# Sixteen-head attention with a mixture of experts: the token stage with the next block's K matmuls between gate/up and down, V and the shift copied by ScalarE, and V stored in rows of 4 KB

## What is computed

```
xn = layernorm(x)                                # no affine part
q, k, v = split(xn @ W_qkv.T + b_qkv)            # 16 heads of 16
probs = softmax(q k^T / 4 - slope_h * |i - j|)
s = (probs @ v) @ W_out.T + b_out
g = silu(routed(xn) + shared(xn))                # 2 of 8 experts, router on xn; one shared expert
shared(xn) = (silu(xn @ sw_gate) * (xn @ sw_up)) @ sw_down
x + s * g
```

## Time and profile before

| | us |
|---|---|
| median of 3 runs (lowest, highest) | 2485.53 (2479.53, 2488.43) |
| the profiled execution: its own time | 2477.84 |
| its span, first to last instruction | 2476.1 |
| the token stage, to the first instruction of the next | 370.6 |
| the attention stage | 370.6 to 2338.8 |
| the output stage | 2338.8 to 2476.1 |
| busy in the span: PE, ACT, DVE, POOL | 2051.5, 1792.6, 1007.1, 549.8 |

### The profile page before, as it was taken

The page is one execution under the profiler, slowest core; times in us unless marked ns, Lnnn a source line. Parts: engine busy times, 40 slices in busy tenths (PEclk is TensorE's granted clock), DMA queues, the critical chain, the costliest instruction groups (busy, mean ns, idle before and its releaser), DMA issues. The chain is left out here.

```text
span 2476.1 us, 41361 instructions
## 1 busy us (share of the span) xinstructions
PE 2051.5 (83%) x15921; PEld 723.3 (29%) x15922; DVE 1007.1 (41%) x2375; ACT 1792.6 (72%) x2080; POOL 549.8 (22%) x577
## 2 busy tenths in 40 slices
PE   4688875676799999999999999999999998788565
PEld 2345542111122224222222332222224221111154
DVE  6676656411133335333333443333335332444255
ACT  3444444566798888888888888888888887888610
POOL 1222220566401111111111111111111104555022
PEclk9888886878899999999999999999999998989888
DMA  9766664554323325332333443233335323433296
GB/s 305 232 212 215 214 204 110 147 155 143 116 74 92 98 78 142 96 86 84 95 96 85 111 114 98 79 94 92 91 87 136 102 63 81 120 103 105 56 285 219
DMA packets 212584, 316.75 MB, mean 128 GB/s; under 512 B 81744, under 2 KB 156112, under 8 KB 212128
## 3 DMA queue, kind: packets, MB, share of 16 engines
q1 hardware_dynamic: 172064, 197.63, 29.1%
q0 software_dynamic: 31872, 108.03, 14.4%
q10 hardware_dynamic: 8448, 8.39, 1.0%
HBM read 196.25 MB, written 125.83 MB: 130 GB/s over the span
## 5 line engine op out<-in xcount | busy, mean ns | idle before, releaser
L1203 ACT ACTIVATE probs_att<-SC_att 128x1024 f32<-128x1024 f32 (+10 forms) x1776 | 1578.0, 956 | 289.0 <-PE SC_att L1093 205.5
L1116 PE MATMUL O_att<-probs_att,V_att 128*32 128x512 f32 (+6 forms) x8192 | 954.1, 535 | 17.1 <-DVE probs_att L1229 15.8
L1093 PE MATMUL SC_att<-Q_att,K_att 64*128 64x512 f16 (+6 forms) x4332 | 654.9, 341 | 241.1 <-ACT probs_att L1203 168.5
L1229 DVE TENSOR_TENSOR probs_att<-probs_att,decay_att 128x128 f32<-128x128 f32 x1024 | 293.5, 291 | 1094.6 <-ACT probs_att L1203 1012.3
L1093 PEld LDWEIGHTS SC_att<-Q_att,K_att 64*128 64x128 f16 (+1 forms) x4332 | 183.2, 94 | 1138.9 <-ACT probs_att L1203 850.2
L1116 PEld LDWEIGHTS O_att<-probs_att,V_att 128*32 128x32 f32 x8192 | 167.6, 110 | 248.6 <-issue 202.3
L1038 POOL DMA_DIRECT2D ys<-ys_att x72 | 51.5, 716 | 743.3 <-DVE ys_att L1276 743.3
L1033 POOL DMA_DIRECT2D xs_att<-xs x72 | 53.3, 740 | 445.6 <-PE TY_att L1137 431.8
L1045 POOL DMA_INDIRECT rows_in_att<-ys,place x128 | 125.5, 981 | 117.5 <-DVE gate_all L1285 83.5
L581 POOL TENSOR_TENSOR parts_tok<-qk_tok,parts_tok 128x512 f16<-128x512 f32 x64 | 78.6, 1230 | 247.0 <-ACT parts_tok L601 242.3
L1023 POOL DMA_INDIRECT xs<-rows_in_att,place x128 | 124.4, 972 | 39.6 <-issue 39.6
(11 more groups left out here) (153 smaller groups left out, 1333.2 us busy)
## 6 DMA issues: line engine op xcount, KB each, us to landing
K_att<-k_stack SPq DMA_DIRECT2D x128, 256.0 KB
Q_att<-q_stack SPq DMA_DIRECT2D x128, 256.0 KB
xs<-zero_tok SPq DMA_DIRECT2D x36, 512.0 KB, 3.8
xs_att<-xs POOLq DMA_DIRECT2D x72, 256.0 KB, 3.2
ys<-ys_att POOLq DMA_DIRECT2D x72, 256.0 KB, 2.6
k_stack<-parts_tok SPq DMA_DIRECT2D x96, 128.0 KB
q_stack<-parts_tok SPq DMA_DIRECT2D x96, 128.0 KB
x_raw_tok<-in_x SPq DMA_DIRECT2D x16, 512.0 KB, 5.7
```

What stands on the lines that cost most here:

```text
L1093: mm = pe.matmul(SC[:, c % SLOTS, at:at + x1 - x0], K[par][side or 0][rows, k * P:(k + 1) * P], Q[par][rows, x0:x1], start=True, stop=True)
L1116: mm = pe.matmul(O[VW * g:VW * (g + 1), par, col:col + width * len(mine)], V[par][:, k, :], spans[:, j0:j0 + BPB * (len(mine) - 1) + 1:BPB ...
L1203: nc.scalar.activation(probs[chunk.step % DEPTH][:, chunk.base:chunk.base + chunk.width], SC[:, c % SLOTS, start:start + chunk.width], ACT ...
L1229: v.tensor_tensor(diag, diag, decay[:, chunk.head, :], ALU.mult).then_inc(faded, 1)
```

## The change

PE runs `own(j)` ahead of `gate_up(j)`, and `k_chunks(j+1)` between `gate_up(j)` and `down(j)`. V's copy out of PSUM and the computation of the shift move from DVE to ACT. The root for block j+2 moves to the start of ACT's block, with a SiLU on one number behind it (`warm_up`); `keep_shared` moves into the next block. On DVE, `gated(j-1)` moves into block j between the two K chunks, `ln_apply` and `ln_stats` move ahead of the Q chunks, and each product follows its own Q chunk. V's bias leaves the token stage: the output stage projects it with `w_o` once, and adds the result to `b_o`. V is stored as 128 rows of 4 KB per block; the load of a head's V then reads four pieces of 256 bytes per partition, where it read one of 1 KB.

The diff, cut to its core:

```diff
@@ tokens_stage
-            (b_v[:], a["b_qkv"].rearrange("(o n) -> o n", o=1)[:, 2 * D:3 * D].broadcast_to([P, D])),
...
-        v_rows = keep["values"].rearrange("(n p) k -> p n k", p=P)
+        v_rows = keep["values"].rearrange("(j p q) k -> j p (q k)", p=P, q=TT)
@@ sync
                     sp.wait_ge(v_out, j + 1)
-                    sp.dma_start(v_rows[:, b * H:(b + 1) * H, g * TT * HD:(g + 1) * TT * HD],
-                                 v_block[:].rearrange("p h t d -> p h (t d)")).then_inc(v_stored, 16)
-                    sp.wait_ge(own_read, j + 1)
+                    sp.dma_start(v_rows[j], v_block[:].rearrange("p h t d -> p (h t d)")).then_inc(v_stored, 16)
+                    sp.wait_ge(shift_ready, j + 1)
@@ tensor
                         pe.wait_ge(own_read, j)
+                        pe.wait_ge(shift_ready, j)
                         pe.wait_ge(logit_out, j)
...
-                    pe.wait_ge(own_ready, j + 1)
+                    pe.wait_ge(own_ready, DC * (j + 1))
...
+                    own(j)
                     gate_up(j)
-                    own(j)
-                    down(j)
                     if j + 1 < NBLK:
                         k_chunks(j + 1)
+                    down(j)
@@ scalar
+                def take_v(j):
+                    act.wait_ge(v_mm, j + 1)
+                    if j > 0:
+                        act.wait_ge(v_stored, 16 * j)
+                    for u in range(2):
+                        ins = nc.scalar.activation(v_block[:, :, 2 * u:2 * u + 2, :], VY[:, u, :].rearrange("p (t h d) -> p h t d", t=2, d=HD),
+                                                   ACT.Copy, scale=undo[:, 0:1])
+                    ins.then_inc(v_out, 1)
+
+                def shift_of(j):
+                    act.wait_ge(own_read, j + 1)
+                    if j > 0:
+                        act.wait_ge(shift_out, 16 * j)
+                    nc.scalar.activation(shift[HALF:HALF + H, :], GU[HALF:HALF + H, 2, :], ACT.Identity, bias=lift[HALF:HALF + H, :],
+                                         scale=SHIFT_AT_Q / SCORE).then_inc(shift_ready, 1)
+
+                def warm_up():
+                    nc.scalar.activation(spare[:], one[:], ACT.Silu)
...
                 for j in range(NBLK):
-                    for k in range(4):
+                    if j + 2 < NBLK:
+                        root(j + 2)
+                        warm_up()
+                    for k in range(2):
+                        split(j, k)
+                    if j > 0:
+                        keep_shared(j - 1)
+                    for k in range(2, 4):
                         split(j, k)
                     square(j)
+                    take_v(j)
                     take_logits(j)
+                    shift_of(j)
                     if j + 1 < NBLK:
                         take_xT(j + 1)
-                    if j + 2 < NBLK:
-                        root(j + 2)
                     gated(j)
-                    keep_shared(j)
+                keep_shared(NBLK - 1)
@@ vector
                 for j in range(NBLK):
-                    for k in range(4):
-                        take_qk(j, k)
-                    products(j)
-                    take_v(j)
+                    take_qk(j, 0)
+                    if j > 0:
+                        gated(j - 1)
+                    take_qk(j, 1)
                     if j + 2 < NBLK:
                         ln_apply(j + 2)
+                    if j + 3 < NBLK:
+                        ln_stats(j + 3)
+                    for c in range(DC):
+                        take_qk(j, 2 + c)
+                        product(j, c)
+                    largest(j)
                     if j + 1 < NBLK:
                         take_xT(j + 1)
-                    gated(j)
-                    shifts_of(j)
-                    if j + 3 < NBLK:
-                        ln_stats(j + 3)
+                gated(NBLK - 1)
@@ attend_stage, load_v
-                    sp.dma_start(V_raw[par][:].rearrange("p t d -> p (t d)"), keep["values"][n * P:(n + 1) * P, :]).then_inc(v_loaded[par], 16)
+                    b, h = divmod(n, H)
+                    src = v_rows[b * BPB:(b + 1) * BPB, :, h * TT * HD:(h + 1) * TT * HD].rearrange("g p k -> p g k")
+                    sp.dma_start(V_raw[par][:].rearrange("p (g t) d -> p g (t d)", g=BPB), src).then_inc(v_loaded[par], 16)
@@ deliver_stage
+                    sp.dma_start(b_v[:], a["b_qkv"].rearrange("(c p) -> p c", p=P)[:, 2 * DC:3 * DC]).then_inc(loaded, 16)
...
+                for c in range(DC):
+                    mm = pe.matmul(Z[:, 1, 1, 0:D], b_v_wide[:, c, :], w_o[:, c, :], start=(c == 0), stop=(c == DC - 1))
+                mm.then_inc(carried, 1)
...
+                v.tensor_copy(b_v_wide[:], b_v[:].unsqueeze(2).broadcast_to([P, DC, P])).then_inc(widened, 1)
                 scale(0)
+                dve.wait_ge(carried, 1)
+                v.tensor_tensor(b_o[:], b_o[:], Z[:, 1, 1, 0:D], ALU.add).then_inc(summed, 1)
+                dve.wait_ge(summed, 1)
```

More of the change, by code:

```diff
@@ L310, in tokens_stage @@
         b_qk = r.sb("b_qk", [P, 2 * DC])
-        b_v = r.sb("b_v", [P, D])
+        one = r.sb("one", [P, 1])
+        spare = r.sb("spare", [P, 1])
+        lift = r.sb("lift", [P, 1])
         x_raw = r.sb("x_raw", [P, 3, TT, D])
@@ L755, in gated, with largest @@
                                            op0=ALU.mult, op1=ALU.mult).then_inc(hid_ready, 1)
-                def shifts_of(j):
+                def largest(j):
                     dve.wait_ge(own_mm, j + 1)
-                    v.tensor_reduce(stat[0:3 * VW, j:j + 1], GU[0:3 * VW, 2, :], AX.X, ALU.max)
-                    if j > 0:
-                        dve.wait_ge(shift_out, 16 * j)
-                    v.tensor_scalar(shift[HALF:HALF + H, :], GU[HALF:HALF + H, 2, :], SHIFT_AT_Q / SCORE, -LIFT * SHIFT_AT_Q,
-                                    ALU.mult, ALU.add).then_inc(own_read, 1)
+                    v.tensor_reduce(stat[0:3 * VW, j:j + 1], GU[0:3 * VW, 2, :], AX.X, ALU.max).then_inc(own_read, 1)
+                v.memset(one[:], 1.0)
+                v.memset(lift[:], -LIFT * SHIFT_AT_Q).then_inc(marks_set, 1)
                 ln_stats(0)
@@ L1457, in deliver_stage @@
         b_o = r.sb("b_o", [P, D])
+        b_v = r.sb("b_v", [P, DC])
+        b_v_wide = r.sb("b_v_wide", [P, DC, P])
         o = r.sb("o", [P, BPB, DC, TB])
@@ L1478, in _ @@
                 sp.dma_start(w_o[:], a["wT_out"].rearrange("(c p) n -> p c n", p=P)).then_inc(loaded, 16)
+                with nc.allow_non_contiguous_dma(reason="256 biases, once"):
+                    sp.dma_start(b_v[:], a["b_qkv"].rearrange("(c p) -> p c", p=P)[:, 2 * DC:3 * DC]).then_inc(loaded, 16)
                 sp.dma_start(b_o[:], a["b_out"].rearrange("(o n) -> o n", o=1).broadcast_to([P, D])).then_inc(loaded, 16)
```

33 lines of the change are left out of this document (15 added, 18 removed).

## The result

The changed kernel is faster, by half of what was forecast: its median is 2468.57 us (2457.24 to 2479.57, 13 runs) against 2488.37 (2475.46 to 2494.03, 13 runs) before, a ratio of 0.9931 with an interval of 0.9911 to 0.9952. The ratio is that of the means, and by them the gain is 0.7 per cent, 17 us, where 33.4 us, 1.3 per cent, was forecast. One of six later executions of the changed kernel took 8817.07 us; it was not profiled, its cause is not known, and it is left out of what follows.

What follows compares the result with a forecast made beforehand. No engine filled a block; TensorE's wait for the shared expert's hidden block and the lowered clock behind it did most. Start +8.1, blocks 2 to 12 -35.1, 13 and 14 -6.4, 15 -1.6, later stages +1.1, +0.5: -33.4, 2452 us, range 2438 to 2470.

Steps and rivals of the forecast that it cites:

- Blocks 13 to 15: Token stage, blocks without statistics: 13 and 14 take 30.8 us against 37.2; block 15 to the next stage 20.1 against 21.7.
- both copies on ScalarE: Work moved to ScalarE in each token block: V's two copies out of PSUM 1.25 us, the shift 0.65 us.
- The start of block 2: Token stage: K of block 2 starts at 96.6 us against 88.49 before, +8.1, bounds +6 and +9.
- The shift's issue: SP's queue in token blocks: 0.5 us behind V's 128 pieces, against 3.47 behind 2048 before.
- V's loads in the attention stage: 512 pieces in place of 128 cost 0.7 us of SP's hold and 0.5 of landing; taken as +1.1, bounds 0 and +3.
- the 32 us: Attention stage: the cost if each of 64 loads of V held its head for 0.5 us; not counted.
- Both terms, 1.1 and 0.5: Costs forecast outside the token stage: attention stage +1.1 us for V's loads, output stage +0.5 for one more small load.
- LayerNorm 1.29: VectorE's chain in each token block: LayerNorm was counted at 1.29 us, within a first loop of 16.9 us.
- the second loop is the raw x: Token blocks, from statistics through shift, zeros and x's landing: 16.8 us, as long as the first loop.
- late x: Rival, chance 0.12: x lands 7.4 us after issue each time in token blocks, costing 18 us, time 2470.
- the waits stay near 1.02 us, at which the clock held: TensorE in token blocks: waits of 1.3 us for squares and 0.8 for the transpose, with the full clock kept.
- That rival: Chance 0.08: the clock falls behind the 1.3 us wait ahead of the sums over heads, costing 24 us, time 2476.

## Why the prediction was right in direction and wrong in size

**Right.** The mechanism: down no longer waits, K has the full clock, the table loads and `keep_shared` are covered. Blocks 13 to 15 (0.9 and 0.8 off), both copies on ScalarE. The start of block 2 is only 1.1 us off, but by luck: K of block 1 came 2.0 us earlier than forecast (77.66 for 79.7), and block 1 took 1.0 longer. The shift's issue takes 0.52 us in the median (0.33 to 1.02) where 0.5 was forecast. For V's loads in the attention stage I had 0.7 us of SP's hold and 0.5 of landing, together 1.1. The hold doesn't show: the issue behind such a load takes 0.46 us in the median where it took 0.45. The landing is 0.5 longer, the first wait for V is 5.42 instead of 5.06, and VectorE waits for V nowhere else. So the 32 us that stood beside the rule of the Trainium skill's "DMA: Bandwidth & Descriptors" (Specifications) on transfers below 512 B, should each of the 64 loads hold its head, aren't there; the stage's +3.2 us is inside the 9.2 us by which it scatters. The output stage's +4.2 doesn't come back on the other chips, where the two kernels without its part of the change took longer (143.9 and 146.8, against 135.3 to 142.1). Both terms, 1.1 and 0.5, are too small for the stages' times to bear out or refute; of the first, the rows show 0.4.

**The step that failed: "LayerNorm 1.29".** I took the row from a place where GpSimd is idle, and moved it to a place where GpSimd subtracts. It is 3.17 there, 1.9 more. The next terms gave some 0.6 back, since I had taken the product from beside GpSimd (1.30), and now the first, the one that the chain goes through, meets none of its subtractions: 0.69. The second, off the chain, takes 0.96. With a few tenths less elsewhere that is 17.87 for 16.9: 10.7 us of the 20.8. With GpSimd held back the row is 1.38 us again, which shows the cause. The Trainium skill's "SBUF — State Buffer", under Who interferes with whom, has the rule: VectorE and GpSimd share a port pair, a `tensor_scalar` in a 2-port mode takes all of it, and the pair is locked for a whole instruction. The trace agrees, with 1.35 and 1.24 us for instructions of 0.4 that end 0.14 and 0.16 us behind GpSimd's. Statistics at 1.41 beside GpSimd agree as well. With this rule the row could have been priced ahead of time: 1.29 and the better part of two subtractions of 1.16.

**The second step: "the second loop is the raw x", 16.8 us.** It is 18.5 in the new kernel, from the statistics at 218.31 to those at 236.83. To the end of the shift (227.17) it is 8.9, where I had 9.6. Then V, the rest of the shift and two DMAs of zeros take SP until 230.31, so 3.1 us and not 1.45:

```profile
228.40 1.86 SPq L456 DMA_DIRECT2D xs<-zero_tok  x2
230.31 2.49 SPq L410 DMA_DIRECT2D x_raw_tok<-in_x  x1
```
```profile
236.83 1.41 DVE L725 BATCH_NORM_STATS2 stats_tok<-x_raw_tok 128x6 f32<-128x256 f32 x4 [0.95 <-DMA x_raw_tok<-in_x]
```

An issue of zeros costs 0.93 us here and cost 0.45 in the earlier trace rows, where it stood behind the hold of 3.47. Two of them take 1.92 us in the median with the change and 1.88 in the old order with V in rows of 4 KB, but 0.90 in both kernels with the small pieces. So what I forecast as 3 us won at the shift's issue was paid back in part, one us a block, at the zeros. x is there 6.5 us after its issue, not 5.7. I held late x for a rival with a chance of 0.12 and a price of 18 us, by a longer landing alone. It was there in six of the eleven blocks, for 8.8 us in all.

**The third: "the waits stay near 1.02 us, at which the clock held".** The wait ahead of the sums over heads was forecast at 1.3. It was 1.96 at the least, up to 4.02 where x was late, and the clock fell in seven of the twelve blocks from 1 to 12. That rival had 0.08. Whether the transposes ahead of the wait matter can't be told, since the router's matmuls, the transposes and the wait stand together in every block of the new order. Late x and the clock are one case, which I should have priced together: a late input lengthens a wait, and the wait costs once more in clock. Their two prices, 24 and 18 us, each came near to what was missing, and so the time, 2468.57, lies within my range of 2438 to 2470. That is luck: the upper end stood for late x alone, and LayerNorm's row, half of the 20.8 us, was in no rival. By the sign that I had set, a period over 18.7, the forecast is wrong: the mean is 18.99.

What bounded the loop was as drawn. With the two causes taken away, by x ahead of the zeros and GpSimd held back, blocks 2 to 12 take 183.3 and 185.8 us where I had 188.1. An undisturbed block takes 16.48 and not 16.9, mostly by the product that I had priced too high. The stage then ends 7.6 to 10.7 us before the forecast 335.6; 5.5 to 5.9 of that are won ahead of block 2, where x of block 3 also comes earlier.

## What to carry over

The duration of a row belongs to its neighbours as much as to its shape: when an instruction is moved, look at what the other engines do at the new place, GpSimd for VectorE above all. When two loops have nearly the same length, shortening one by itself gives little (5.1 and 10.6 us alone, 25.1 to 28.1 together). And a wait ahead of light TensorE work should be priced with the clock that it may cost.
